# Feed-forward pass of a vision transformer block: from two chunks to four in two groups, with layers 3 and 4 on halves of the array

## What is computed

```python
h = tok_ref(x, W, b)                       # 128 images, 196 patches of 768 -> 256
h = concatenate([cls_tok, h], axis=1)      # 197 tokens
h = h + attn_ref(layernorm(h), ...)
h = h + ffn_ref(layernorm(h), ...)

# ffn_ref
gf = global_net(x.mean(axis=1))            # per image: 256 -> 128 -> 64 -> 1, sigmoid
out = x
for _ in range(3):
    tf = coupling_net(out)                 # per token: 256 -> 256 -> 128 -> 64 -> 1, gelu, sigmoid
    coupling = 0.1 + adaptive_range * (0.7 * gf + 0.3 * tf - 0.5) * 2.0
    out = out + coupling * twist(out)      # twist permutes and negates quarters of the features
```

## Time and profile before

| | |
|---|---|
| median of 3 runs | 4171.35 us (4170.29 to 4171.71) |
| the profiled execution's own time | 4168.86 us |
| its span, first to last instruction | 4167.1 us |
| mean granted clock of TensorE | 0.993 |
| busy: PE, DVE, ACT, POOL | 94%, 73%, 60%, 44% of the span |
| DMA | 398.36 MB, mean 96 GB/s |
| chain that ended last | PE 62%, DVE 28%, ACT 1% |

### The profile page before, as it was taken

The page is one execution under the profiler, slowest core; times in us unless marked ns, Lnnn a source line. Parts: engine busy times, 40 slices in busy tenths (PEclk is TensorE's granted clock), DMA queues, the critical chain, the costliest instruction groups (busy, mean ns, idle before and its releaser), DMA issues.

```text
span 4167.1 us, 82613 instructions
## 1 busy us (share of the span) xinstructions
PE 3923.4 (94%) x29199; PEld 2685.7 (64%) x29454; DVE 3043.7 (73%) x7070; ACT 2484.6 (60%) x5890; POOL 1852.6 (44%) x2960
## 2 busy tenths in 40 slices
PE   6999999999999999999999999879999999999998
PEld 4777777777777777777777777744444444444444
DVE  6777777777777777777777777656776777777776
ACT  4666666666666666666666666634444444444443
POOL 3666666666666666666666666510000000000000
PEclk9999999999999999999999999989999999999999
DMA  3444444444444444444444444311111111111111
GB/s 96 120 120 120 120 120 121 120 120 120 120 121 120 121 119 119 119 119 119 119 119 119 119 119 119 98 57 47 59 59 47 62 55 50 61 54 51 62 52 39
DMA packets 281756, 398.36 MB, mean 96 GB/s; under 512 B 27778, under 2 KB 232067, under 8 KB 281347
## 3 DMA queue, kind: packets, MB, share of 16 engines
q1 hardware_dynamic: 281346, 393.07, 35.7%
HBM read 132.06 MB, written 53.26 MB: 44 GB/s over the span
## 4 chain that ended last, share of the span: by engine, by line
PE 62%; DVE 28%; another core or an unknown queue 5%; issue 3%; ACT 1%; DMA 0%; POOL 0%; DVEq 0%; SPq 0%; POOLq 0%
PE ps L1014 17%; PE ps L1276 13%; DVE mx L848 12%; PE ps L1092 7%; DVE mx L844 7%; PE ps L1285 7%; PE ps L1294 4%; DVE k L823 3%; PE ps L1290 3%; PE ps L1053 3%; PE ps L1100 3%; ACT a L672 1%; DVE st L774 1%; PE ps L1307 1%
## 5 line engine op out<-in xcount | busy, mean ns | idle before, releaser
L1014 PE MATMUL ps<-w_tok,xb 128*128 128x256 f32 (+1 forms) x3072 | 834.0, 395 | 0.9 <-ACT qkv L540 0.5
L526 POOL TENSOR_SCALAR ve<-mv 128x4 f32<-128x4 f32 x64 | 14.8, 232 | 1287.5 <-DVE mv L897 1287.5
L1276 PE MATMUL ps<-X,cn_w 128*128 128x394 f32 x1536 | 552.3, 502 | 0.0
L546 ACT ACTIVATE p<-ps 128x394 f32<-128x394 f32 x1024 | 454.4, 499 | 127.1 <-PE ps L1053 127.1
L848 DVE TENSOR_REDUCE mx<-ps 69x2 f32<-69x396 f32 x1024 | 528.5, 555 | 0.0
L1014 PEld LDWEIGHTS ps<-w_tok,xb 128*128 128x128 f32 (+1 forms) x3072 | 449.7, 165 | 81.6 <-issue 1.3
L844 DVE TENSOR_REDUCE mx<-ps 128x4 f32<-128x512 f32 x512 | 350.7, 685 | 202.7 <-remote 202.7
L664 ACT ACTIVATE a<-ps,cn_b 128x394 f32<-128x394 f32 x384 | 226.2, 589 | 368.0 <-PE ps L1276 354.2
L1053 PE MATMUL ps<-qZ,kT 128*128 128x396 f32 (+1 forms) x2048 | 398.6, 328 | 5.5 <-DMA qZ<-mx_scratch 5.5
L1124 PE MATMUL ps<-kZ,qT 128*69 128x396 f32 x1024 | 394.6, 452 | 0.3 <-DVE h L767 0.3
L1276 PEld LDWEIGHTS ps<-X,cn_w 128*128 128x128 f32 x1536 | 279.9, 190 | 176.2 <-issue 2.8
(11 more groups left out here) (137 smaller groups left out, 8468.5 us busy)
## 6 DMA issues: line engine op xcount, KB each, us to landing
kZ<-kT SPq DMA_DIRECT2D x512, 198.0 KB, 3.4
qZ<-qT SPq DMA_DIRECT2D x256, 396.0 KB, 4.8
xb<-in_x SPq DMA_DIRECT2D x128, 588.0 KB, 6.6
h_scratch<-h SPq DMA_DIRECT2D x128, 128.0 KB
hl<-h_scratch SPq DMA_DIRECT2D x64, 256.0 KB
hk<-h_scratch SPq DMA_DIRECT2D x64, 256.0 KB
out<-hk SPq DMA_DIRECT2D x64, 256.0 KB
h_scratch<-h SPq DMA_DIRECT2D x128, 69.0 KB
```

Source lines behind the costliest of these rows:

```text
L546: s.activation(p0[:, i, 2 * jj:2 * jj + 2, :], ps[:, (b0, b1)[jj], 0:2 * TE].rearrange("p (a b) -> p a b", b=TE)[:, :, 0:T], ACT.Exp).then ...
L1014: mm = t_.matmul(ps[:M, W[t], 0:D], xb[:, par, k, t * P:t * P + M], w_tok[:, k, :], start=k == 0, stop=k == KT - 1)
L1276: mm = t_.matmul(ps[:, 4 * c + mt, 0:N2], cn_w1[:, f, mt * P:mt * P + P], X[:, c, state(cyc), f, :], start=f == 0, stop=f == FT - 1)
```

## The change

Four chunks in two groups (0, 1 and 2, 3), so eight images make a quad and there are 16 (`QUADS`). A phase is one cycle of one group's layers 1 and 2, together with layers 3 and 4, tanh and `update` of the other group's last cycle (`phases`). Layer 3 of a group's two chunks writes rows 0 to 63 and 64 to 127 of one bank, through two column halves of the array, so one gelu serves both; layer 4 reads rows 0 to 63 and 64 to 127 through two row halves and writes two banks. `cn_w4`, `cn_w4r` and `cn_b3` are held twice for that. A chunk now owns two banks, which layers 1 to 4 and the transposes share. `base` is made in a step of its own (`bases`) at the start of a phase. `qkv` is moved to the part of SBUF that is given free after the first pass. The gate network runs once for a group (four images). SP's order is new as well. The diff, cut to its core:

```diff
         cn_w3 = sb("cn_w3", [F2, F3])
-        cn_w4 = sb("cn_w4", [F3, 1])
-        cn_w4r = sb("cn_w4r", [F3, P])
+        cn_w4 = sb("cn_w4", [2 * F3, 1])
...
+        QUADS = B // 8
+
+        def phases():
+
+            for i in range(QUADS):
+                for cyc in range(CYCLES):
+                    for G in range(2):
+                        oi, ocyc = (i, cyc) if G else (i, cyc - 1) if cyc else (i - 1, CYCLES - 1)
+                        yield i, cyc, G, oi, ocyc
...
-            def store_and_next_hk(i):
-                for c in range(2):
+            def store_and_next_hk(i, G):
+                for c in (2 * G, 2 * G + 1):
                     store_out(i, c)
-                    sp.wait_ge(out_stored[c], i * 32 + 32)
-                    load2(hk, i + 1, c, hk_loaded)
-
-            if PAIRS > 1:
-                next_hl(1)
-                for i in range(PAIRS - 2):
-                    next_hl(i + 2)
-                    store_and_next_hk(i)
-                store_and_next_hk(PAIRS - 2)
-            for c in range(2):
-                store_out(PAIRS - 1, c)
-            for c in range(2):
-                sp.wait_ge(out_stored[c], 32 * PAIRS)
+                if i + 1 < QUADS:
+                    for c in (2 * G, 2 * G + 1):
+                        sp.wait_ge(out_stored[c], i * 32 + 32)
+                        load2(hk, i + 1, c, hk_loaded)
+
+            for G in range(2):
+                next_hl(1, G)
+            for i in range(QUADS):
+                store_and_next_hk(i, 0)
+                if i + 2 < QUADS:
+                    next_hl(i + 2, 0)
+                store_and_next_hk(i, 1)
+                if i + 2 < QUADS:
+                    next_hl(i + 2, 1)
+            for c in range(4):
...
+                if oi >= 0:
+                    gelu3(oi, ocyc, O)
+                    if fresh:
+                        gnet(oi + 1, O, 1)
+                gelu1(i, cyc, 2 * G)
+                if oi >= 0:
+                    for c in (2 * O, 2 * O + 1):
+                        tanh(oi, ocyc, c)
+                    if fresh:
+                        gnet(oi + 1, O, 2)
+                gelu1(i, cyc, 2 * G + 1)
+                if oi >= 0 and ocyc == 1 and oi + 1 < QUADS:
+                    for c in (2 * O, 2 * O + 1):
+                        x_copy(oi + 1, c)
+                gelu2(i, cyc, 2 * G)
+                if cyc == CYCLES - 1 and i + 1 < QUADS:
+                    gnet(i + 1, G, 0)
+                gelu2(i, cyc, 2 * G + 1)
...
+            def bases(i, cyc, c):
+                G, e = divmod(c, 2)
+                old = X[:, c, state(cyc)]
+                dve.wait_ge(alpha_ready[G], i + 1)
+                if cyc == 0:
+                    dve.wait_ge(x_ready[c], i * 2 + 2)
+                else:
+                    dve.wait_ge(x1_new[c], i * CYCLES + cyc)
                 for f, op in ((0, ALU.add), (1, ALU.subtract)):
                     for im in range(2):
                         cols = slice(im * T, im * T + T)
                         v.scalar_tensor_tensor(base[:, c, f, cols], old[:, 1 - f, cols],
-                                               alpha[:, c, im:im + 1], old[:, f, cols], ALU.mult, op)\
-                         .then_inc(base_ready[c], 1)
-                dve.wait_ge(l_ready[c], n * 5)
-                v.scalar_tensor_tensor(u0[:, c, :], old[:, 1, :], c_tf[:, 0:1], th[:, c, :], ALU.mult, ALU.mult)\
-                 .then_inc(u0_ready[c], 1)
-                if cyc == 0 and not first:
+                                               alpha[:, G, 2 * e + im:2 * e + im + 1], old[:, f, cols],
+                                               ALU.mult, op).then_inc(base_ready[G], 1)
+
...
-            def pass2(i, prev, nxt):
-                if prev:
-                    finish(i - 1, 0)
-                    update(i - 1, 1, CYCLES - 1, False)
-                    alphas(i, 1)
-                    finish(i - 1, 1)
-                update(i, 0, 0, not prev)
-                if nxt:
-                    stats2(i + 1, 0)
-                    stats2(i + 1, 1)
-                    apply2(i + 1, 0, False)
-                update(i, 1, 0, not prev)
-                if nxt:
-                    apply2(i + 1, 1, False)
-                update(i, 0, 1, False)
-                if nxt:
-                    gsums(i + 1, 0)
-                update(i, 1, 1, False)
-                if nxt:
-                    gsums(i + 1, 1)
-                update(i, 0, 2, False)
-                if nxt:
-                    alphas(i + 1, 0)
-
...
+            for i, cyc, G, oi, ocyc in phases():
+                O = 1 - G
+                pair = (2 * O, 2 * O + 1)
+                if oi >= 0:
+                    for c in pair:
+                        bases(oi, ocyc, c)
+                if i + 1 < QUADS:
+                    if cyc == 0:
+                        for c in (2 * G, 2 * G + 1):
+                            stats2(i + 1, c)
+                    elif cyc == 1:
+                        if G == 0:
+                            for c in (0, 1):
+                                apply2(i + 1, c, False)
+                        else:
+                            for c in (2, 3):
+                                apply2(i + 1, c, False)
+                    elif cyc == 2:
+                        for c in (2 * G, 2 * G + 1):
+                            gsums(i + 1, c)
+                if oi >= 0:
+                    for c in pair:
+                        update(oi, ocyc, c)
+                    if ocyc == CYCLES - 1:
+                        if oi + 1 < QUADS:
+                            alphas(oi + 1, O)
+                        for c in pair:
+                            finish(oi, c)
...
+            def layer1(i, cyc, c, f):
+                if cyc:
+                    pe.wait_ge((x0_new, x1_new)[f][c], i * CYCLES + cyc)
+                elif f == 0:
...
+            def layer3(i, cyc, G):
+                for e in range(2):
+                    pe.wait_ge(a2_ready[2 * G + e], i * CYCLES + cyc + 1)
+                for e in range(2):
+                    mm = t_.matmul(ps[e * F3:e * F3 + F3, 4 * G + 1, 0:N2], cn_w3[:], a2[:, 2 * G + e, :],
+                                   start=True, stop=True, tile_position=(0, e * F3))
+                mm.then_inc(l3_done[G], 1)
+
+            def layer4(i, cyc, G):
+                pe.wait_ge(a3_ready[G], i * CYCLES + cyc + 1)
+                for e in range(2):
+                    rows = slice(e * F3, e * F3 + F3)
+                    t_.matmul(ps[:, 4 * G + 3 * e, 0:N2], cn_w4r[rows, :], a3[rows, G, :], start=True, stop=True)\
+                      .then_inc(l4_done[G], 1)
...
-            def pass2(i, prev, nxt):
-                for cyc in range(CYCLES):
-                    last = nxt and cyc == CYCLES - 1
-                    layer(i, 0, cyc, 0, prev, nxt)
-                    if last:
-                        gnet(i + 1, 0, 0)
-                    if cyc == 0 and prev:
-                        gnet(i, 1, 2)
-                        y_transpose(i - 1, 0, True)
-                    if cyc or prev:
-                        layer(i if cyc else i - 1, 1, (cyc - 1) % CYCLES, 2)
-                    layer(i, 0, cyc, 1, prev)
-                    if cyc or prev:
-                        layer(i if cyc else i - 1, 1, (cyc - 1) % CYCLES, 3)
-                    layer(i, 0, cyc, 2, prev, nxt)
-                    layer(i, 0, cyc, 3)
-                    if nxt and cyc == 1:
-                        x_transpose(i + 1, 0)
-                    if last:
-                        gnet(i + 1, 0, 1)
-                    if cyc == 0 and prev:
-                        y_transpose(i - 1, 1, True)
-                    layer(i, 1, cyc, 0, prev, nxt)
-                    if last:
-                        gnet(i + 1, 1, 0)
-                    layer(i, 1, cyc, 1, prev)
-                    if nxt and cyc == 1:
-                        x_transpose(i + 1, 1)
-                    if last:
-                        gnet(i + 1, 0, 2)
-                        gnet(i + 1, 1, 1)
...
+            for i, cyc, G, oi, ocyc in phases():
+                O = 1 - G
+                there_ = oi >= 0
+                fresh = ocyc == CYCLES - 1 and oi + 1 < QUADS
+                layer1(i, cyc, 2 * G, 0)
+                if there_:
+                    if fresh:
+                        pe.wait_ge(g_ready[O], oi * 3 + 4)
+                    layer3(oi, ocyc, O)
+                    if fresh:
+                        gnet(oi + 1, O, 1)
+                layer1(i, cyc, 2 * G, 1)
+                if there_:
+                    layer4(oi, ocyc, O)
+                layer1(i, cyc, 2 * G + 1, 0)
+                if there_ and fresh:
+                    gnet(oi + 1, O, 2)
+                layer1(i, cyc, 2 * G + 1, 1)
+                if there_ and ocyc == 1 and oi + 1 < QUADS:
+                    for c in (2 * O, 2 * O + 1):
```

(99 more changed lines are left out.)

271 lines of the change are left out of this document (104 added, 167 removed).

## The result

Slower: 4289.52 us (median of 4 runs, 4285.62 to 4294.40) against 4171.53 us, a ratio of 1.028 [1.027, 1.030]. The forecast was 4220 us, so the sign was right and the loss, 118 us, more than twice the 48 us forecast. The profiled execution took 4294.40 us, its span 4292.6.

The account below looks back on a forecast made before the run. PE, 92% busy, bounds the old pass; in the new one the late hl load makes a quad 94.5 us against 88.6. 14 x 94.5 = 1323 plus edges makes 1476.5 against 1428, +48: 4220 us, range 4077 to 4296.

Parts of the forecast that it names:

- The place of the loss: DVE at bn_stats, right behind finish, waits for the late hl load: 28 waits of about 10 us.
- the store lands in 4.0 us (mean of 60 waits): First term of the chain from the end of finish(c1): 4.0 us until the store lands, before further loads are issued.
- The steps of 2.7 us: Loads in a burst: each further chunk's load lands 2.7 us after the one before.
- A: First phase of a quad, cycle 0 of group 0: 27 us with the late load, 17.8 of it to the statistics' end.
- The bound: Upper end of the chain from finish to the statistics' end: 20.5 us, one more chunk's 2.7 on top of 17.8.
- The burst of loads: Reloads of hk and loads of hl behind the landed store: 13.8 us from landing to the end of statistics.
- The phases: Six phases of a quad, one per cycle and group: 70.6 us in all if no load is late.
- Full overlap of the halves: Packed layer 3 and layer 4 products run side by side on PE, so a phase is 14 products of 0.66 us.
- The clock: PE at half clock after idling: eight layer-1 records take 4.61 instead of 2.8 us, a transpose of eight 1.94 instead of 1.06.
- rival 4: PE's clock doesn't fall in the waits: 3.4 us less a quad, 4172 us; chance 0.05.
- C's wait: PE waits for DVE's X at the start of the phase of cycle 1, group 0: 8 to 12 us.
- Start and end: Edges of the pass: quad 0 65 us, quad 15 65.5, the last group's remainder 17, a start 6 later.

Follow-up runs that it names:

- experiment 1: Changed kernel with SP's loads of hl for the quad after next, both groups, issued ahead of the stores: 3872.31 us, ratio 0.929.
- experiment 10: Changed kernel with only group 0's hl loaded ahead of its stores, group 1's still after its own: 4079.95 us, ratio 0.978.
- experiment 5: Changed kernel with only the stores' 69-row DMAs cut into 64 and 5 rows, loads whole: 4196.05 us, ratio 1.006.
- experiment 7: experiment 1's kernel with each pair of layer 3 and of layer 4 issued twice: 3992.55 us, ratio 0.957.
- experiment 8: Changed kernel with PE kept busy in its two long waits of each quad by products that nothing reads: 4279.26 us, ratio 1.026.
- experiment 6: Changed kernel with only the loads' 69-row DMAs cut into 64 and 5 rows, stores whole: 4167.35 us, ratio 0.999.
- experiment 4: Kernel before the change with its loads of hl moved behind the stores and the reload of hk: 4488.93 us, ratio 1.077.

## Why the prediction went wrong

- **The place of the loss**: right. The wait is where it was forecast, at the statistics behind finish; experiment 1 removes it and its 417 us, experiment 10 half of it.
- **The step that failed**: "the store lands in 4.0 us (mean of 60 waits)". Measured were 7.95 and 6.1 us. The 4.0 us is a wait of a kernel that issues one chunk's store and waits for it before anything else, counted from the end of the issue. In the new order two stores go out behind each other, and SP waits for the second. The same timeline of the kernel before had the right number: from the first issue of a store at 3317.50 to the reload that it releases it is 4.76 us:

```profile
3322.26 0.77 SPq L379 DMA_DIRECT2D hk<-h_scratch  x2
```

Two in a row from the first one's start make 9.5 us; finish(c1) ends 1.8 us after that start (3406.1 against 3404.33), so 7.7, and measured were 7.95. Finish(c3) ends 3.0 us after the first store's start (mean), so 6.5, and measured were 6.1. This sum was made after the result; what experiment 5 shows is that the whole 69-row stores make the landing late. The steps of 2.7 us were added for each load but none for the first store; the 1.4 us put in for hk c0 and "the first store still in the same engines' way" went into the burst of loads, not into the landing. 94.5 + 3.95 + 2.1, less 0.7 in A's rest and 0.1 in each burst, make the 99.6 us measured.
- **The bound**: 20.5 us as the chain's upper end was too low for A (21.6). It came from one more step of 2.7 us, a load's, while a store's is 4.6 behind finish(c1). That 4289.5 us still lies inside the stated range is luck: the mean chain, 20.7 us, is above the bound too, and A's shorter rest made up for it.
- **The burst of loads**: right, 13.7 us from landing to the end of statistics against 13.8 (with the 1.4 us in it); 14.5 in experiment 5, where the stores are out of its way sooner.
- **The phases**: right. Without the wait the quad is 69.6 us (forecast 70.6), A 13.5 (13.5), the rest 56.1 (57.1). Full overlap of the halves was right as well (experiment 7).
- **The clock**: it fell, as forecast, but rival 4's 3.4 us a quad was too much. Experiment 8 gets 10 us back in all, 0.7 a quad: shorter steps of PE between the two stores of a group are lost in the queue. It restored the clock only in part behind C's wait, so the full price stays open.
- **Start and end**: of the pass, 6 us more than forecast (159 against 153.5; the pass takes 1553.6, less 14 x 99.6).

The forecast was carried by one chain whose terms came from a kernel that never had two stores under way; with 28 passes through it, 3 us are 84 us of the total.

## What to carry to other kernels

When a change restructures the work, look first at where each load is issued against the store that it queues behind: here moving the load ahead of the stores is worth 417 us, over three times the packing's 120. Price a chain of DMAs by the number that are in the queues when it starts, and count from the first one's issue; a wait measured for a lone store is a lower bound. And where two stores queue, counting from the first one's issue, an engine that delivers the second one's data sooner gains little.

## What the runs showed that was not expected

- Cutting a copy of 69 rows into 64 and 5 lets a group's second store land 3.2 us after finish instead of 7.95 (experiment 5), and shortens the time from landing to the end of statistics from 13.7 to 9.5 us (experiment 6), though SP issues half as many DMAs again (some 0.5 us each).
- A store of 128 + 69 rows has a longer step in the queue than a load of the same size: second stores landed 4.6 us behind the first after finish(c1) and 4.2 after finish(c3) (means of 14), hl of c1 2.75 us behind that of c0 (3423.22 to 3425.97). The reload of hk c0, which is issued between the two landings, isn't what makes it: with the loads cut (experiment 6) the steps are still 4.4 and 4.1 us. Why a store takes longer was not tried.
- The slow clock behind waits of 12 to 16 us gave back only some 0.7 us a quad when PE was kept busy in them (experiment 8); behind the wait of 7.7 us in experiment 4 it costs 2.7 us a pair.
